# TensorE products of zeros at the starts of the Mamba, ternary and attention stages

## The reference

```python
x = x + 0.5 * _L0_ffn_ref(_layernorm(x), ...)   # mixture of 8 experts, top 2, and a shared one
x = x + _L0_attn_ref(_layernorm(x), ...)        # Mamba, forward and reversed, 16 states
x = x + 0.5 * _L0_ffn_ref(_layernorm(x), ...)   # the mixture again
x = x + 0.5 * _L1_ffn_ref(_layernorm(x), ...)   # five linear layers with weights -1, 0, 1
x = x + _L1_attn_ref(_layernorm(x), ...)        # causal attention, 16 heads of 8
x = x + 0.5 * _L1_ffn_ref(_layernorm(x), ...)   # the five linear layers again
```

## Time and profile before

| what | value |
|---|---|
| median of 3 runs | 2819.32 us (2819.30 to 2819.78) |
| the profiled execution's own time | 2823.07 us |
| its span, first to last instruction | 2821.0 us |
| PE busy | 2458.8 us (87%) |
| DVE busy | 2216.2 us (79%) |
| ACT busy | 1698.4 us (60%) |
| POOL busy | 1432.5 us (51%) |
| mean granted TensorE clock | 0.947 |

### The profile page before, as it was taken

The page is one execution under the profiler, slowest core; times in us unless marked ns, Lnnn a source line. Parts: engine busy times, 40 slices in busy tenths (PEclk is TensorE's granted clock), DMA queues, the critical chain, the costliest instruction groups (busy, mean ns, idle before and its releaser), DMA issues. The chain is left out here.

```text
span 2821.0 us, 35553 instructions
## 1 busy us (share of the span) xinstructions
PE 2458.8 (87%) x10516; PEld 1557.5 (55%) x10516; DVE 2216.2 (79%) x4289; ACT 1698.4 (60%) x2971; POOL 1432.5 (51%) x1482
## 2 busy tenths in 40 slices
PE   6998487878889888877799499979999999997999
PEld 5776243333334434324677388855555555546887
DVE  7998489989999999998899555458877777755444
ACT  3676566557656666643578365536776767764555
POOL 2474698888888988884277450033232323310000
PEclk8999698999999999999899799979999999998999
DMA  2256222222222222222157310000000000001000
GB/s 76 62 163 117 84 75 71 73 68 75 68 72 75 75 76 72 75 77 67 28 136 146 97 40 1 0 16 1 1 1 1 2 1 1 1 1 42 8 8 15
DMA packets 99496, 146.05 MB, mean 52 GB/s; under 512 B 13036, under 2 KB 50540, under 8 KB 99124
## 3 DMA queue, kind: packets, MB, share of 16 engines
q1 hardware_dynamic: 82196, 98.60, 11.5%
q0 software_dynamic: 16608, 44.78, 7.3%
q10 hardware_dynamic: 512, 0.53, 0.1%
HBM read 124.98 MB, written 18.87 MB: 51 GB/s over the span
## 5 line engine op out<-in xcount | busy, mean ns | idle before, releaser
L1756 POOL TENSOR_TENSOR a_hc<-a_H,a_cb 128x512 f32<-128x512 f32 x512 | 620.3, 1233 | 134.7 <-DVE a_H L1619 127.1
L1411 PE MATMUL a_Y<-a_hc,ident 128*128 128x512 f32 x1024 | 543.7, 642 | 57.9 <-POOL a_hc L1756 49.8
L2112 ACT ACTIVATE a_pt<-a_W 128x512 f32<-128x512 f32 (+3 forms) x768 | 346.2, 496 | 202.1 <-PE a_W L2012 198.3
L1537 ACT ACTIVATE a_dA<-a_dt,a_aneg 128x512 f32<-128x512 f32 x512 | 342.8, 715 | 191.7 <-POOL a_dt L1775 100.2
L1411 PEld LDWEIGHTS a_Y<-a_hc,ident 128*128 128x128 f32 x1024 | 185.7, 198 | 312.0 <-POOL a_hc L1756 216.5
L1643 DVE TENSOR_TENSOR a_BX<-a_u,a_BX 128x1024 f32<-128x1024 f32 x256 | 308.7, 1211 | 35.7 <-PE a_BX L1345 24.9
L1619 DVE TENSOR_TENSOR_SCAN a_H<-a_dA,a_H,a_BX 128x512 f32<-128x512 f32 x256 | 312.4, 1263 | 3.6 <-ACT a_dA L1537 3.6
L2335 POOL TENSOR_SCALAR_AFFINE_SELECT a_pt<-a_pt 128x512 f32<-128x512 f32 x128 | 91.1, 712 | 422.8 <-ACT a_pt L2112 422.8
L1619 DVE TENSOR_TENSOR_SCAN a_H<-a_dA,a_BX 128x512 f32<-128x512 f32 x256 | 296.7, 1203 | 0.9 <-POOL a_hc L1756 0.9
L2198 DVE CUSTOM_DVE_ANT_0 a_masked<-a_W,a_mask 128x384 f32<-128x384 f32 (+3 forms) x512 | 231.8, 487 | 80.5 <-PE a_W L1999 78.4
L2012 PE MATMUL a_W<-a_Q,a_K 128*128 128x512 f32 (+3 forms) x768 | 283.6, 385 | 1.7 <-ACT a_pt L2112 1.6
(11 more groups left out here) (323 smaller groups left out, 5444.6 us busy)
## 6 DMA issues: line engine op xcount, KB each, us to landing
a_cb<-a_crow SPq DMA_DIRECT2D x256, 256.0 KB, 3.2
m_orows<-m_yt SPq DMA_DIRECT2D x46, 256.0 KB, 2.5
t_wst<-ternary_w SPq DMA_DIRECT2D x22, 256.0 KB, 2.7
m_xrows<-m_xn SPq DMA_DIRECT2D x16, 256.0 KB, 2.3
m_xg<-m_xrows,m_gidx POOLq DMA_INDIRECT x184
out<-x SPq DMA_DIRECT2D x8, 256.0 KB, 2.3
m_wg<-moe_ws SPq DMA_DIRECT2D x2, 516.0 KB, 4.5
a_hc<-mamba_conv_rows SPq DMA_DIRECT2D x1, 1024.0 KB, 5.1
```

The source lines that it names most:

```text
L1411: pe.matmul(Y[:, h, :], ident[:], hc[:, g % HCRING, :], start=False, stop=v == NS - 1).then_inc(s_y, 1)
L1537: act.activation(dA[:, G % ARING, :], dt[:, b % 2, h, :], ACT.Exp, scale=aneg[:, d, h, v:v + 1]).then_inc(s_dA, 1)
L1756: pool.tensor_tensor(hc[:, G % HCRING, :], H[:, s, span], cb[:, v % RING, :], ALU.mult).then_inc(s_hc, 1)
L2112: act.activation(pt[:, u % PR, 0:BLK - r * P], W[:, 3 + u % 3, 0:BLK - r * P], ACT.Exp).then_inc(s_exp, 1)
```

## The change

A helper is added that makes n float32 products of the identity with the first 512 columns of zeros behind the tokens, and it is called on PE in these places:

- Mamba: 21 products before the wait for s_pad, behind a new wait until both weight casts are done (s_wh at 2), and 4 between the first transposes and the first convolution product. They write bank 0 of BX.
- Ternary: before the first transposes 26 products with `back`, behind a new wait for two split weights (s_wsp at 2), or 5 without `back` and without a new wait; 4 behind these transposes in both; with `back` also 3 before the second block's transposes and 9 behind them. They write bank 0 of Y.
- Attention: 7 before the first transposes, 6 before the second, 3 before the first keys. They write PV.

Nobody reads these products; their banks are written anew before they are used. Nothing is removed, and no other engine's stream changes.

```diff
--- before.py
+++ after.py
@@ -83,6 +83,11 @@
         last = dve.bn_aggr(mv[:, t, :], stats[:, t, :])
     return last
 
+
+
+def products_of_zeros(pe, n, out, x, ident):
+    for _ in range(n):
+        pe.matmul(out, ident[:], x[:, TOKENS:TOKENS + BLK], start=True, stop=True)
 
 
 class Returned:
@@ -860,7 +865,11 @@
                                 passes(U[:, n % 4, :], v, k, a, xh[:, a, :], xl[:, a, :], True, True)\
                                     .then_inc(s_up, 1)
                             if k == after:
+                                if back:
+                                    products_of_zeros(pe, 3, Y[:, 0, :], x, ident)
                                 norm_T(0, 1)
+                                if back:
+                                    products_of_zeros(pe, 9, Y[:, 0, :], x, ident)
                         else:
                             n = first_prod[s, a] + k
                             bank_free(pe, i, n)
@@ -898,7 +907,11 @@
                 def pair(i, first=False):
                     for a in range(2):
                         if first and a == 0:
+                            if back:
+                                pe.wait_ge(s_wsp, 2)
+                            products_of_zeros(pe, 26 if back else 5, Y[:, 0, :], x, ident)
                             norm_T(0, 0)
+                            products_of_zeros(pe, 4, Y[:, 0, :], x, ident)
                             pe.wait_ge(s_wsp, 2)
                         stage(i, 0, a, after=SECOND_T if first and a == 0 else None)
                         if not first:
@@ -1414,6 +1427,8 @@
                 for b in range(-1, NB + 1):
                     uses = uses_of(b)
                     if b == -1:
+                        pe.wait_ge(s_wh, 2)
+                        products_of_zeros(pe, 21, BX[:, 0, :], x, ident)
                         pe.wait_ge(s_pad, 4)
                     if b == 0:
                         pe.wait_ge(s_pre, 3)
@@ -1421,6 +1436,7 @@
                         rows(0, 1)
                     for v in range(NS):
                         if (b, v) == (-1, 1):
+                            products_of_zeros(pe, 4, BX[:, 0, :], x, ident)
                             pe.wait_ge(s_wl, 2)
                         if (b, v) == (-1, 5):
                             pe.wait_ge(s_ld, 16 * len(LOADS))
@@ -2073,6 +2089,8 @@
                     G = i * GROUPS + g
                     uses = slot_uses(stage, g)
                     for v in steps(stage):
+                        if v < -4:
+                            products_of_zeros(pe, {-7: 7, -6: 6, -5: 3}[v], PV[:], x, ident)
                         if v == -5:
                             pe.wait_ge(s_pre, 2)
                         for j in range(GH):
```

## The result

The changed kernel takes 2848.22 us (median of 4 runs, 2848.17 to 2848.29) against 2819.55 us for the kernel before: a ratio of 1.0098 with a 95% interval of 1.0082 to 1.0114. It is slower by 28.7 us. The forecast was 2845.4, in a range of 2838 to 2855. The profiled execution of the changed kernel took 2848.29 us at a span of 2846.1 us, and the one of before 2823.07 us, 3.5 more than its median, so the two profiled executions lie 25.2 us apart (25.1 by their spans).

A forecast was written before the change was run, and what follows sets the result against it. At the stage starts PE was taken to stand on a chain through DVE, POOL and ACT, so its lateness passes on. 8.3 + 15.1 + 1.6 + 1.1 = 26.1 us on 2819.32 gave 2845.4 us, range 2838 to 2855.

The forecast's parts named there:

- What a product costs: Each helper call on PE is two float32 records 0.43 us apart, so 0.86 us at full clock, 1.71 at 1.2 GHz.
- Rival 1: Everywhere: a product costs half or less, one record; only the clock's returns stay, 9.1 us faster, 2810.2 us; chance 0.05.
- When the clock rises: At low-clock starts PE runs 3.9 us (2.9 to 5.6) at half clock, so n products take n x 0.86 + 3.9 / 2.
- rival 2: Everywhere: zeros don't raise the clock, so every product costs 1.71 us; 2924 us; chance 0.03.
- Mamba: Start of Mamba: first convolution product 9.9 us later, less 1.65 for 12 faster matmuls: +8.3 us (7.7 to 9.2).
- Rival 3: Half of the lateness is eaten behind it, in Mamba by DVE's loop catching up; 13 us, 2833 us; chance 0.05.
- First ternary stage: First group +12.4 us, second block's first matmul +17.0, less 1.9 for its slow matmuls: +15.1 us (13.8 to 16.9).
- Attention: Attention start: first transposes on time at full clock, second +1.8 us; stage +1.6 us (0 to 3).
- the kept case: Attention's first transposes: if the clock falls on the way, the seven products end at 1874.4, after the rows at 1873.55.
- Second ternary stage: First group 3.5 us later, 2.4 given back by the warm clock: +1.1 us (0.5 to 2.5).
- The sum: All four starts: 8.3 + 15.1 + 1.6 + 1.1 = 26.1 us, bounds 22 to 31.6, clock dips some 2 us either way.

The follow-up runs named there:

- fitted counts: Changed kernel with counts cut to Mamba 10, 1; first ternary 12, 1, 1, 4; attention 6, 3, 2; second ternary 2, 1: 2814.90 us against 2822.53 before.
- the eight more in Mamba: Kernel with fitted counts plus 8 more products in Mamba's block -1 (4, 3 and 1): 2808.75 us against 2819.27 for the kernel before.
- slope run: Changed kernel with 16 products instead of 21 in Mamba and 20 instead of 26 in the first ternary stage: 2838.48 us against 2819.27 for the kernel before.

## Why the prediction was right, point by point

*What a product costs.* Right, and it decided all. 0.86 us was read from L1411's two records a call; the helper has 184 records for 92 calls, and halving the columns alone makes the change a gain. Rival 1 (half the price) is the result of that experiment: 2815.7, where before took 2822.5 on the same chip. The prediction puts 0.86 us beside the four passes of the Trainium skill ("FP8 and Floating Point Precision", TensorE Precision Notes). That section names the passes and no time; the figure is an estimate, four times the 0.216 us, and the price in the sum comes from the rows of L1411.

*When the clock rises.* The clock did rise on zeros, so rival 2 falls. The slow stretch was set at 3.9 us for every place. It was 3.7 in Mamba (293.5 to 297.2) and 5.7 in the first ternary stage (1595.4 to 1601.1), just outside the end of 5.6 that was kept. Over all kernels here it lay between 2.9 us (Mamba, fitted counts) and 6.2 (first ternary stage, with the eight more in Mamba), so no one value fits all starts.

*Mamba.* Forecast +8.3 (7.7 to 9.2), measured +10.0 by the stage's length in the first pair of traces, outside that range, and +6.8 with Mamba's products alone. Up to ACT's first read of O it is +8.1. Another 0.6 to the first scan was not in the sum: behind the products the clock falls at another moment (331.3 to 345.0) and of the first twelve convolution products of the second rows all run slow, where nine did before. But without products in Mamba this part varies from 53.2 to 54.9 us, so the 0.6 is within its spread. The last 1.2 us lie in the loop between first scan and stage's end, 966.0 us, against 962.8 to 965.3 in the other traces; they have no cause that I can show. Rival 3, half of the lateness eaten, falls: some 4 us would have to be caught up in the loop, and late by 8 to 9 us it took 966.0 and, with Mamba's products alone, 963.0 us, while with 256 columns, where nothing was late, it took 962.8. Less than its own spread of 2.5 us can't be excluded.

*First ternary stage.* Forecast +15.1, measured +15.9. The term that was too small is the slow stretch at its start: 12.2 us late at the transposes, where 11.1 were forecast. The second block's first matmul came +17.6 (forecast +17.0), and 1.7 were returned by the clock (forecast 1.9). The forecast's own terms for this block add up to 1635.8, not 1635.5, which would have made it +17.3.

*Attention.* The start behaved as worked out: first transposes 1.0 late, since the clock fell for one stretch after all (the kept case), second +2.7 for a forecast of +1.8, the 1.0 included, first scores +1.7. With the same 7, 6 and 3 products in the slope run the clock did not fall before the first transposes, and they were on time. That the stage grew by 1.6 us can't be shown: its length varies by 4 us.

*Second ternary stage.* Transposes +2.3 (forecast +2.25), first group +3.2 (+3.5), DVE's second product +1.1, stage +1.0 (+1.1).

*The sum.* 26.1 forecast, 28.7 between the medians. The stated range is a little wider than the sum's bounds with 2 us on either side, which are 2839 to 2853; the result lies in both. By the two traces Mamba is 1.7 over its forecast and the first ternary stage 0.8. Against these stand the attention stage, 1.9 under, and the mixture stages, 1.5 shorter; but the trace of before was 3.5 us longer than its median, and its second trace has the mixture stages 1.6 and 1.9 shorter, so I put the 2.6 us that were missing down to Mamba and the first ternary stage as likely, not as shown. That the total comes so near is in part luck, since single stages were off by 0.1 to 1.9 us in both directions. The chance of 0.94 on slower rested on one row and one count in the code, and both held.

## What to carry to other kernels

Price an added instruction by counting its records per call in the trace, not by the look of one record: a plain float32 matmul is two records here, and a filler that looks half as long as it is turns a gain of 7 us into a loss of 29. Filler in front of a chain must end before the first rows come, since PE works in order and what is over is handed through to the end of the stage, less the some 2 us that the raised clock gives back (1.7 and 2.2 in the two ternary stages): twice the products in the attention stage made its first scores 11 to 12 us late and the stage 10 to 14 us longer. Fitted to the gaps the filler does pay: 0.2% at the four starts (0.1 to 0.3%), and 0.4% (0.2 to 0.5%) with the second dip in Mamba filled too.

## What the runs showed of the hardware

Products with zeros as the moving operand raise TensorE's clock like others: it went from 0.50 to 1.00 under them after 3.7 us in one place and after 5.7 in another, where matmuls of real data had taken 3.6 and 5.5.

The idle time before a start alone doesn't tell whether the clock falls. Before the attention stage of the changed kernel PE had been idle for 1.50 us, and its first 14 records there took 7.92 us, where full clock would make it 13 x 0.43 + 0.59 = 6.2: the 1.7 more are half of some 3.4 us at half clock. In the slope run the same 14 records behind the same 1.50 us took 6.25 us, at full clock:

```profile
1878.44 6.25 PE L90 MATMUL a_PV<-x,ident 128*128 128x512 f32 x14 [1.50 <-PEq L67]
```

One chip ran the unchanged kernel in 2908 us where others took 2819 to 2822, with the two mixture stages and the first ternary stage 32, 30 and 20 us longer and the rest within 2 us. These three gather rows by DMA, but so does the Mamba stage (L104, 64 times), which was only 1.3 us longer, so the gathers alone do not explain it. Its cause was not looked for.
